# First stage in overlapping rounds, the second stage's weights split at its head, and the last expert's share of the first batch added by products

## The chip, the cores and the metric

The kernel runs on one core of a Trainium2 chip. The metric is the device time of one execution in microseconds, the median of the runs shown; lower is better. TensorE multiplies and transposes into eight PSUM banks, VectorE, ScalarE and GpSimd work element by element (GpSimd works on SBUF alone), and transfers are issued from the queues of SyncE (SP), ScalarE and GpSimd.

## The reference, cut to what matters

Four batches of 512 tokens of 256 numbers pass two decoder layers, six stages in all, each followed by adding the input and a layer norm. The change touches the first four:

```
x = norm(x + spectral(x))       # stage 1: filter from x, bits of a latent, a Golay correction
x = norm(x + gated(x, ctx))     # stage 2: cross attention both ways, weights Wq_c .. Wv_c, Wg
x = norm(x + experts(x))        # stage 3: 8 experts, 512 given tokens each, gelu MLP
x = norm(x + self_attention(x)) # stage 4: rope, 16 heads

# stage 1, per batch, x1 = x @ C, with C a 256x256 matrix from x's extremes and box counts
bits = (x1 @ W_el + b_el > 0); syn = (bits @ H.T > 0.5); w = syn.sum()
bits = where(0 < w <= 3, mod(bits + syn, 2), bits);  y = x1 + bits @ W_le + b_le
# stage 3: out[tok] += weight * (gelu(x[tok] @ W1 + b1) @ W2 + b2), tokens may repeat
```

## The kernel before, in words

Every engine has its own instruction stream, written out in Python, and works through it in order; semaphores (`Signal`, `Bank`) order the engines. X holds all 2,048 tokens in 16 tiles of 128; a batch is 4 tiles (a quarter). Precise products are made from a high and a low part (fp32r pairs), three products for one: ScalarE writes the high part, and VectorE or GpSimd subtracts it for the low part.

**Stage 1** (`spectral`, lines 239 to 528). Small tables and x come in; VectorE finds the extremes (L401, L402) and with a logarithm and sines on ScalarE (L384, L386) the filter, from which TensorE makes C and C W_el (L317, L323). Meanwhile the seven weights of stage 2 pass through two staging buffers (SP, L286, each load behind the subtraction two names earlier), are copied by ScalarE (`take_weights`) and subtracted by GpSimd (L505), three before the rounds and two in each of the next; the context of batch 0 comes last. Then TensorE loops over k = 0 to 4 (L325 on): transposes of batch k+1, latent of batch k (L334), result products of batch k-1 (L344, L345), syndrome (L351) and weight (L354) of batch k. VectorE's loop has bits and flip (L456, L458), threshold (L460), the sums (L466), statistics and aggregates (L472, L476) of batch k-1, three operations of the correction (L480 to L486) and the norm of batch k-1 (L490), for which GpSimd makes the root (L519, L521).

**Stage 2** (`gated`). Before its loop stand the transposes of batch 0 (L596), VectorE's bias scalings, and the split of the source in `take_source(0)` (ScalarE L722, VectorE L814). Then TensorE makes the projections of batch 0 (all L585).

**Stage 3** (`mixture`). Per expert: gather 512 rows, up products with gelu, down products (L1040), weighting (L1200, L1202), a merge product that sums repeated tokens inside a tile of 128 (L1066), its copy (L1172), and a scatter with addition into `acc_scratch` in DRAM (GpSimd, L1231), each scatter behind the one before it. The stage ends with a barrier of all engines but GpSimd.

**Stage 4** (`self_heads`). Wq, Wk, Wv come in through two buffers that rope uses later (SP L1803), ScalarE copies, VectorE subtracts (L1643), then scales bq (L1645) and sets Vone to zero (L1646). The four quarters of the sums are loaded when the last scatter has landed (`norm_loads`, two on each queue), then come statistics, root and norm (`average`, `root`, `norm`) of batch 0, transposes (L1399), copies (L1564), rope (L1664 on VectorE, L1769 on GpSimd), the source's split (L1571, L1672), projections (L1391), and hops over DRAM that bring the heads into rows. GpSimd sets two rows each of rows_q and rows_k (L1772, L1773). Batches 1 to 3 are normed later (`of_next(s, 38)`).

## Time and profile before

| | |
|---|---|
| median of 3 runs | 1976.09 us (1973.51 to 1984.03) |
| the profiled execution's own time | 1980.55 us |
| its span, first to last instruction | 1979.2 us |
| PE, DVE, ACT, POOL busy | 84%, 58%, 51%, 50% of the span |
| mean granted TensorE clock | 0.928 of full speed |

A timeline line gives start, busy time, engine, line, operation, tiles and shapes, and in brackets how long the engine was idle before it and what ended that. Neighbouring instructions of one kind are merged (x4 is four). PE is TensorE's matmul, PEld its weight load, DVE VectorE, ACT ScalarE, POOL GpSimd; ACTq and SPq are the queues that issue transfers. An fp32 product counts as two records. A granted clock of 1.00 is 2.4 GHz and 0.50 is 1.2 GHz.

### The profile page before, as it was taken

The page shows a single profiled execution, that of the slowest core. Times are in us where ns is not written, and L with a number is a line of the kernel's source. Part 1 is how long each engine was busy: PE and PEld are TensorE (multiplying, and loading weights), DVE is VectorE, ACT ScalarE, POOL GpSimd, SP SyncE. Part 2 cuts the span into 40 slices and gives each one's busy share as a digit, 9 for nine tenths or more (in the row PEclk, how much of TensorE's full clock was granted, in tenths as well). Part 3 has the DMA queues.
Part 4 walks back from the last instruction along what each step waited for, and adds up shares of the span by engine and source line. Part 5 has one row for each costly group of instructions (what it writes and reads, how often), then busy time and mean ns, then how long its engine had stood idle before and what let it go on. Part 6 is the DMA issues. An engine that isn't in the chain of part 4 may idle for free. (4 is left out here: it accounts for less than half of the span.)

```text
span 1979.2 us, 23648 instructions
## 1 busy us (share of the span) xinstructions
PE 1667.1 (84%) x7419; PEld 1216.5 (61%) x7419; DVE 1148.9 (58%) x2237; ACT 1012.4 (51%) x1933; POOL 983.2 (50%) x832
## 2 busy tenths in 40 slices
PE   5699994999953897979988999989999997589892
PEld 2387773778842575757655666656666665566661
DVE  4766664666645685858746665655665572542223
ACT  2154442654521485757784776666676673232222
POOL 1200002243324475767873775665675583068885
PEclk9899997999986799999998999999999998579996
DMA  2300103444335222323020111020121120248777
GB/s 83 129 11 1 33 22 101 129 127 133 73 87 137 64 67 64 76 60 81 22 98 15 31 39 31 25 65 23 33 63 26 27 59 19 63 110 192 180 183 173
DMA packets 96785, 146.15 MB, mean 74 GB/s; under 512 B 22711, under 2 KB 61820, under 8 KB 93830
## 3 DMA queue, kind: packets, MB, share of 16 engines
q1 hardware_dynamic: 66448, 104.92, 18.5%
q0 software_dynamic: 18432, 26.36, 7.5%
q10 hardware_dynamic: 11782, 13.37, 2.2%
q8 instruction: 61, 1.00, 0.2%
q14 instruction: 62, 0.51, 0.1%
HBM read 101.83 MB, written 36.41 MB: 70 GB/s over the span
## 5 line engine op out<-in xcount | busy, mean ns | idle before, releaser
L2288 POOL TENSOR_TENSOR STp_lo_use<-ST_use,STp_hi_use 128x512 fp32r<-128x512 f32 x256 | 337.7, 1328 | 201.0 <-ACT ST_use L2118 199.5
L1764 POOL TENSOR_TENSOR STp_lo<-ST,STp_hi 128x512 fp32r<-128x512 f32 x192 | 248.1, 1312 | 104.5 <-ACT ST L1539 103.2
L2183 DVE TENSOR_REDUCE nmax_use<-bank 128x1 f32<-128x512 f32 x256 | 173.6, 680 | 110.0 <-PE bank L2023 105.4
L2114 ACT ACTIVATE STp_hi_use<-bank 128x512 fp32r<-128x512 f32 x256 | 153.1, 598 | 161.0 <-PE bank L2049 157.2
L1657 DVE TENSOR_REDUCE nmax<-bank 128x1 f32<-128x512 f32 x256 | 171.0, 684 | 51.1 <-PE bank L1453 50.2
L1453 PE MATMUL bank<-rows_k,rows_q 65*128 65x512 f32 x256 | 134.8, 535 | 38.8 <-DVE nmax L1657 21.5
L2118 ACT ACTIVATE ST_use<-bank 128x512 f32<-128x512 f32 x256 | 151.7, 593 | 2.0 <-POOL STp_lo_use L2288 2.0
L1536 ACT ACTIVATE STp_hi<-bank 128x512 fp32r<-128x512 f32 x192 | 116.8, 608 | 57.9 <-PE bank L1464 57.4
L2023 PE MATMUL bank<-ks,qs 128*128 128x512 f32 x256 | 110.5, 432 | 10.2 <-DMA ks<-ks 9.6
L1539 ACT ACTIVATE ST<-bank 128x512 f32<-128x512 f32 x192 | 117.8, 613 | 0.0
L951 POOL TENSOR_SCALAR veps<-mv 128x4 f32<-128x4 f32 x4 | 0.9, 228 | 229.2 <-DVE mv L888 229.2
L2730 POOL DMA_INDIRECT acc_scratch<-res,sidx_all x64 | 102.0, 1593 | 24.2 <-issue 17.4
L2033 PE MATMUL bank<-qs,ks 128*128 128x512 f32 x256 | 103.2, 403 | 9.2 <-DMA q<-rowbuf_use 9.0
L1464 PE MATMUL bank<-rows_q,rows_k 66*128 66x512 f32 x256 | 106.3, 415 | 0.9 <-ACT ST L1539 0.8
L2047 PE MATMUL bank<-STp_hi_use,V_hi 128*65 128x512 f32 x256 | 101.5, 397 | 2.2 <-POOL STp_lo_use L2288 2.2
L2712 POOL DMA_INDIRECT rows<-tokens_scratch,gidx_all x64 | 66.4, 1037 | 74.2 <-DVE sidx_all L2604 55.0
L2034 PE MATMUL bank<-q,k 65*128 65x512 f32 x256 | 102.0, 398 | 0.0
L2049 PE MATMUL bank<-STp_lo_use,V_hi 128*65 128x512 f32 x256 | 101.2, 395 | 0.0
L2048 PE MATMUL bank<-STp_hi_use,V_lo 128*64 128x512 f32 x256 | 101.0, 395 | 0.0
L1453 PEld LDWEIGHTS bank<-rows_k,rows_q 65*128 65x128 f32 x256 | 51.6, 203 | 79.5 <-DVE nmax L1657 44.0
L2699 DVE TENSOR_SCALAR res<-bank,rows 128x256 f32<-128x256 f32 x64 | 28.0, 480 | 118.6 <-DMA acc_scratch<-res,sidx_all 110.2
L1121 ACT ACTIVATE hT_hi<-bank,b 128x512 fp32r<-128x512 f32 x64 | 44.1, 689 | 95.1 <-PE bank L1040 91.6
(444 smaller groups left out, 4633.7 us busy)
## 6 DMA issues: line engine op xcount, KB each, us to landing
stage<-in_W SPq DMA_DIRECT2D x16, 1024.0 KB, 4.9
Wgu<-in_Wgu SPq DMA_DIRECT2D x32, 384.0 KB
rows_q<-hop_scratch SPq DMA_DIRECT2D x32, 256.0 KB, 4.4
ks<-ks SPq DMA_DIRECT2D x64, 128.0 KB, 2.3
rinv<-rinv_scratch SPq DMA_DIRECT2D x64, 128.0 KB, 3.0
rows_k<-hop_scratch SPq DMA_DIRECT2D x24, 256.0 KB, 5.4
hop_scratch<-qkp_hi SPq DMA_DIRECT2D x20, 256.0 KB
Wda<-in_Wdn SPq DMA_DIRECT2D x32, 128.0 KB
```

What stands on the lines that cost most here:

```text
L1453: PE.matmul(bk.ap, rows_q[0:MAX_ROW, h, j * P:(j + 1) * P], rows_k[0:MAX_ROW, h, :], start=True, stop=True).then_inc(bk.full, 1)
L1464: PE.matmul(bk.ap, rows_k[:, h, kt * P:(kt + 1) * P], rows_q[:, h, :], start=True, stop=True).then_inc(bk.full, 1)
L1536: A.activation(parts_of(u)[0], bk.ap, ACT.Exp)
L1539: A.activation(ST[u % TB], bk.ap, ACT.Exp).then_inc(bk.free, 1)
L1657: V.tensor_reduce(nmax[:, i % 2, h % HS * TB + j:h % HS * TB + j + 1], bk.ap, AX.X, ALU.max, negate=True).then_inc(bk.free, 1)
L1764: G.tensor_tensor(parts_of(u)[1], ST[u % TB], plain(parts_of(u)[0]), ALU.subtract).then_inc(low.sem, low.inc(u))
L2023: PE.matmul(bk.ap, qs[z][:, j * P:(j + 1) * P], ks[z], start=True, stop=True).then_inc(bk.full, 1)
L2033: PE.matmul(bk.ap, ks[z][:, kt * P:(kt + 1) * P], qs[z], start=True, stop=False)
L2114: A.activation(STp[u % NHI][0], bk.ap, ACT.Exp)
L2118: A.activation(ST[u % NFULL], bk.ap, ACT.Exp).then_inc(bk.free, 1)
L2183: V.tensor_reduce(nmax[:, (h % 2) * TB + j:(h % 2) * TB + j + 1], bk.ap, AX.X, ALU.max, negate=True).then_inc(bk.free, 1)
L2288: G.tensor_tensor(STp[u % NHI][1], ST[u % NFULL], plain(STp[u % NHI][0]), ALU.subtract).then_inc(low["pool"].sem, low["pool"].inc(u))
```

## The change

Stage 1's loop body is cut into functions with the same instructions: `latent`, `syndrome`, `weight` and `result(k, t)` (one tile) on TensorE, `take_bits`, `take_syndrome`, `correct`, `add(k, z)` (two tiles), `average` and `norm` on VectorE. They are put in a new order, in which batch k+1's bits are made between the tiles of batch k. xT has three buffers. Batches 0 and 1 are transposed before the logarithm. The seven weights have a place each, in the staging room of the experts' weights, and all loads are issued at once; GpSimd's subtractions all come behind the filter. Batch 0's transposes and split for stage 2 move into stage 1's rounds 2 and 3, batch 3's statistics and norm into stage 2's first round.

In stage 3, batch 0's sums of experts 0 to 6 are loaded to X while expert 7 runs, and expert 7's share is added by products of a 0/1 matrix `spread` (token of the row against place in the batch) with the weighted rows: three tiles as pairs, the fourth in fp32. The last scatter moves into stage 4. There VectorE does batch 0's statistics and norm between the weights, the memset of Vone is halved, with its second half behind the source's split, and the loads of quarters 1 to 3 are all issued by SP. New tensors: `spread`, `wvp`, `places` (0 to 511).

```diff
@@ -226,17 +226,25 @@
-    kit.names2 = ("Wq_c", "Wk_s", "Wv_s", "Wq_s", "Wk_c", "Wv_c", "Wg")
+    kit.names2 = ("Wk_s", "Wv_s", "Wq_c", "Wq_s", "Wk_c", "Wv_c", "Wg")
-    kit.stage = [sb("stage%d" % z, [P, 2 * DC, D]) for z in range(2)]
+    room = [kit.stage0["W1"].rearrange("p c f -> p (c f)"), kit.stage0["W2"].rearrange("p c d -> p (c d)")]
+    kit.stage2 = {}
+    for n, name in enumerate(kit.names2):
+        size = 2 * DC * D if name == "Wg" else DC * D
+        kit.stage2[name] = room[n // 4][:, n % 4 * DC * D:n % 4 * DC * D + size].rearrange("p (c d) -> p c d", d=D)
-    kit.staged2 = [Signal(kit, "staged%d" % z, range(4), step=16) for z in range(2)]
+    kit.staged2 = [Signal(kit, "staged%d" % z, kit.names2[3 * z:3 + 4 * z], step=16) for z in range(2)]
...
@@ -276,22 +284,25 @@
             for n, name in enumerate(names2):
-                if n > 1:
-                    SP.wait_ge(w_low2.sem, w_low2[names2[n - 2]])
-                SP.dma_start(stage[n % 2][:, 0:2 * DC if name == "Wg" else DC, :], T[name]).then_inc(staged2[n % 2].sem, staged2[n % 2].inc(n // 2))
-            SP.dma_start(kit.ctxT, T["ctxT"][0]).then_inc(kit.ctx_in.sem, kit.ctx_in.inc(0))
+                if n == 3:
+                    SP.dma_start(kit.ctxT, T["ctxT"][0]).then_inc(kit.ctx_in.sem, kit.ctx_in.inc(0))
+                SP.dma_start(stage[name], T[name]).then_inc(staged2[n // 3 > 0].sem, staged2[n // 3 > 0].inc(name))
...
@@ -307,6 +318,7 @@
             turn(0)
+            turn(1)
...
@@ -322,36 +334,57 @@
...
+            latent(0)
+            turn(2)
+            syndrome(0)
+            weight(0)
+            for k in range(B):
                 if k + 1 < B:
+                    latent(k + 1)
+                result(k, 0)
+                result(k, 1)
+                if k + 1 < B:
+                    syndrome(k + 1)
+                if k == 0:
+                    turn(3)
+                if k == B - 2:
+                    turn(0, "next")
+                result(k, 2)
+                if k + 1 < B:
+                    weight(k + 1)
+                result(k, 3)
...
@@ -362,38 +395,37 @@
-                    if b > 1:
-                        A.wait_ge(bank[6].full, bank[6].full_at["y", b - 2])
-                    A.activation(xT[b % 2][:, c, :], bank[c].ap, ACT.Copy).then_inc(bank[c].free, 1)
+                    if b > 2:
+                        A.wait_ge(bank[6].full, bank[6].full_at["y", b - 3])
+                    A.activation(xT[b % 3][:, c, :], bank[c].ap, ACT.Copy).then_inc(bank[c].free, 1)
-                n = names2.index(name)
-                here = stage[n % 2][:, 0:2 * DC if name == "Wg" else DC, :]
-                A.wait_ge(staged2[n % 2].sem, staged2[n % 2][n // 2])
+                here, z = stage[name], names2.index(name) // 3 > 0
+                A.wait_ge(staged2[z].sem, staged2[z][names2[-1 if z else 2]])
...
             a_own = kit.own["act"]
-            take_weights("Wq_c")
-            take_weights("Wk_s")
+            for name in names2[0:3]:
+                take_weights(name)
+            A.wait_ge(kit.ctx_in.sem, kit.ctx_in[0])
+            A.activation(kit.ctxp[0], kit.ctxT, ACT.Copy).then_inc(kit.ctx_high.sem, kit.ctx_high.inc(0))
             take(0)
+            take(1)
...
             A.activation(trig[:, 4:8], trig[:, 0:4], ACT.Sin).then_inc(logged.sem, logged.inc("sines"))
-            take_weights("Wv_s")
-            take(1)
-            take_weights("Wq_s")
-            take_weights("Wk_c")
+            for name in names2[3:]:
+                take_weights(name)
             take(2)
-            take_weights("Wv_c")
-            take_weights("Wg")
-            A.wait_ge(kit.ctx_in.sem, kit.ctx_in[0])
-            A.activation(kit.ctxp[0], kit.ctxT, ACT.Copy).then_inc(kit.ctx_high.sem, kit.ctx_high.inc(0))
...
             take(3)
+            for c in range(DC):
+                A.wait_ge(bank[c].full, bank[c].full_at["next", 0])
+                A.activation(kit.xp[0][:, c, :], bank[c].ap, ACT.Copy).then_inc(kit.src_high2.sem, kit.src_high2.inc((0, "x%d" % c)))
...
@@ -449,47 +481,78 @@
+            V.wait_ge(kit.bias_in.sem, kit.bias_in["bias0"])
+            for d in range(2):
+                V.tensor_scalar(kit.bq[:, d, :], kit.bias0[:, 3 * d, :], D ** -0.5, None, ALU.mult)
+            V.tensor_scalar(kit.bgh, kit.bias0[:, 6, :], 0.5, None, ALU.mult).then_inc(own.sem, own.inc("bias halves"))
...
+            kit.average1, kit.norm1 = average, norm
+            take_bits(0)
+            take_syndrome(0)
+            correct(0)
+            for k in range(B):
+                if k + 1 < B:
+                    take_bits(k + 1)
                 if k:
+                    norm(k - 1)
+                if k == B - 1:
+                    for c in range(DC):
+                        V.wait_ge(kit.src_high2.sem, kit.src_high2[0, "x%d" % c])
+                        V.tensor_tensor(kit.xp[1][:, c, :], bank[c].ap, plain(kit.xp[0][:, c, :]), ALU.subtract).then_inc(bank[c].free, 1)
+                if k + 1 < B:
+                    take_syndrome(k + 1)
+                add(k, 0)
+                if k + 1 < B:
+                    correct(k + 1)
+                add(k, 1)
+                if k + 1 < B:
+                    average(k)
...
@@ -500,21 +563,14 @@
-            for name in names2[0:3]:
+                G.tensor_tensor(W2[name][1], stage[name], plain(W2[name][0]), ALU.subtract).then_inc(w_low2.sem, w_low2.inc(name))
+
+            G.wait_ge(basis_set.sem, basis_set["gbasis"])
+            G.tensor_tensor(kit.ctxp[1], kit.ctxT, plain(kit.ctxp[0]), ALU.subtract).then_inc(kit.ctx_low.sem, kit.ctx_low.inc(0))
+            for name in names2:
                 take_weights(name)
             for b in range(B):
-                if b == 1:
-                    for name in names2[3:5]:
-                        take_weights(name)
-                if b == 2:
-                    for name in names2[5:]:
-                        take_weights(name)
-                    G.wait_ge(kit.ctx_high.sem, kit.ctx_high[0])
-                    G.tensor_tensor(kit.ctxp[1], kit.ctxT, plain(kit.ctxp[0]), ALU.subtract).then_inc(kit.ctx_low.sem, kit.ctx_low.inc(0))
...
@@ -600,6 +658,9 @@
+                    if k == 0:
+                        PE.wait_ge(*kit.source_taken[c])
+                        continue
...
-            turn(0)
...
-            take_source(0)
...
-            take_source(0)
             for k in range(B + 1):
                 if k < B:
                     take_projections(k, 0)
+                if k == 0:
+                    kit.average1(B - 1)
...
                     over_sum(k, 0, TB - 1)
+                if k == 0:
+                    kit.norm1(B - 1)
...
                 if k == 1:
                     SP.dma_start(kit.acc_d[1], bass.AP(T["zeros"].tensor, 0, [[0, (B * S + CAP) * D // 4096], [1, 4096]])).then_inc(kit.zeros_in.sem, kit.zeros_in.inc("zeros"))
+                    SP.wait_ge(w_low.sem, w_low[kit.names2[-1]])
...
             def group(out, pairs):
+                if e == E0 - 1:
+                    spread_out()
                 merge(e, CT0 - 1)
+
+            def spread_out():
+
+                PE.wait_ge(spread_set.sem, spread_set[CT0 - 2])
+                for j in range(TB):
+                    PE.wait_ge(bank[j].free, bank[j].use(("first", j)))
+                    for t in range(CT0 - 1):
+                        for p in range(2):
+                            PE.matmul(bank[j].ap[:, 0:D], spread[:, t, j * P:(j + 1) * P], wvp[p][:, t, :], start=t == 0 and p == 0, stop=False)
+                PE.wait_ge(weighted.sem, weighted[E0 - 1, CT0 - 1])
+                for j in range(TB):
+                    PE.matmul(bank[j].ap[:, 0:D], plain(spread[:, CT0 - 1, j * P:(j + 1) * P]), wv[(CT0 - 1) % 2], start=False, stop=True).then_inc(bank[j].full, 1)
...
+            for t in range(CT0 - 1):
+                A.wait_ge(weighted.sem, weighted[E0 - 1, t])
+                A.activation(wvp[0][:, t, :], wv[t % 2], ACT.Copy).then_inc(wv_high.sem, wv_high.inc(t))
...
+            def find_places(t):
+
+                if t == 0:
+                    V.wait_ge(tok_in[0].sem, tok_in[0]["places"])
+                m = V.tensor_scalar(spread[:, t, :], tok_row[0], tok_col[:, (E0 - 1) * CT0 + t:(E0 - 1) * CT0 + t + 1], None, ALU.is_equal)
+                if t == CT0 - 1:
+                    m.then_inc(spread_set.sem, spread_set.inc("places"))
+
+            def take_low(t):
+                V.wait_ge(wv_high.sem, wv_high[t])
+                V.tensor_tensor(wvp[1][:, t, :], wv[t % 2], plain(wvp[0][:, t, :]), ALU.subtract).then_inc(spread_set.sem, spread_set.inc(t))
...
+                else:
+                    for t in range(CT0):
+                        find_places(t)
...
                     if t > 1:
                         V.wait_ge(bank[6 + t % 2].full, bank[6 + t % 2].full_at["merge", e, t - 2])
+                        if e == E0 - 1:
+                            V.wait_ge(spread_set.sem, spread_set[t - 2])
...
                     if t:
                         take_merged(e, t - 1)
+                        if e + 1 == E0:
+                            take_low(t - 1)
+                if e + 1 == E0:
+                    V.wait_ge(first_in.sem, first_in["s3"])
+                    for j in range(TB):
+                        V.wait_ge(bank[j].full, bank[j].full_at["first", j])
+                        V.tensor_tensor(X[:, j, :], bank[j].ap[:, 0:D], X[:, j, :], ALU.add).then_inc(bank[j].free, 1)
                 take_merged(e, CT0 - 1)
...
-                for t in range(CT0):
+                for t in range(CT0 - (e == E0 - 1)):
                     bk = bank[6 + t % 2]
                     G.wait_ge(bk.free, bk.free_at["merge", e, t])
+                    if e == E0 - 1 and t == 0:
+                        G.wait_ge(first_in.sem, first_in["s3"])
...
+            SP.wait_ge(own.sem, own["again", E0 - 2])
+            SP.dma_start(tok_row[0], bass.AP(T["places"].tensor, 0, [[0, P], [1, S]])).then_inc(tok_in[0].sem, tok_in[0].inc("places"))
+            SP.wait_ge(stored.sem, stored[E0 - 2, CT0 - 1])
+            SP.dma_start(X[:, 0:TB, :], acc_d[0:S].rearrange("(t p) d -> p t d", p=P)).then_inc(first_in.sem, first_in.inc("s3"))
...
+        last = bank[6 + (CT0 - 1) % 2]
+        kit.last_merged = last.free, last.free_at["merge", E0 - 1, CT0 - 1]
+        kit.first_added = [(bank[j].free, bank[j].free_at["first", j]) for j in range(TB)]
...
-            norm_loads(A, (1, 3))
...
         def average(k):
-            V.wait_ge(kit.quarter_in[k].sem, kit.quarter_in[k]["s3"])
+            if k:
+                V.wait_ge(kit.quarter_in[k].sem, kit.quarter_in[k]["s3"])
             for t in range(NT)[quarter[k]]:
+                if k == 0:
+                    V.wait_ge(*kit.first_added[t])
...
@@ -1638,14 +1753,19 @@
-            for n, name in enumerate(names):
...
+            average(0)
+            take_weights(0)
+            norm(0)
+            take_weights(1)
+            take_weights(2)
             V.wait_ge(kit.tables_in.sem, table)
             V.tensor_scalar(bq, bqkv[:, 0, :], HD ** -0.5, None, ALU.mult).then_inc(own.sem, own.inc("s4 bias"))
-            V.memset(plain(Vone), 0.0).then_inc(own.sem, own.inc("s4 V"))
-            average(0)
-            norm(0)
+            V.memset(plain(Vone[:, 0:TB // 2]), 0.0)
...
+                if of_next(s, 26) == 0:
+                    V.memset(plain(Vone[:, TB // 2:TB]), 0.0).then_inc(own.sem, own.inc("s4 V"))
...
@@ -1751,8 +1873,12 @@
         def pool():
+            root(0)
+            G.wait_ge(*kit.last_merged)
+            G.wait_ge(kit.stored0.sem, kit.stored0[E0 - 1, CT0 - 2])
+            G.indirect_dma_start(kit.acc_d[0], bass.IndirectOffsetOnAxis(ap=kit.last_sidx[:, CT0 - 1:CT0], axis=0), summed[:, CT0 - 1, :], None,
+                                 compute_op=ALU.add).then_inc(kit.stored0.sem, kit.stored0.inc((E0 - 1, CT0 - 1)))
             G.wait_ge(kit.tables_in.sem, table)
-            root(0)
...
-            norm_loads(SP, (0, 2))
+            norm_loads(SP, (1, 2, 3))
```

## Rows read from the trace of the kernel before

**Rows 1.** Busy time by stretch: length, PE, PEld, DVE, ACT, POOL, granted clock, DMA share, GB/s.

```profile
98.00:108.00 10.00, 10.00 (x48) 8.38 (x48) 3.59 (x5) 3.36 (x5) 0.00 (x0) 0.84 0.01 2
...
637.00:690.00 53.00, 45.14 (x121) 26.82 (x122) 36.75 (x62) 22.02 (x41) 18.42 (x14) 0.68 0.31 74
```

**Rows 2.** Timeline of the first stage: start, length, engine, operation, idle before.

```profile
21.01 0.20 ACT L384 ACTIVATE mm<-mm 5x1 f32<-5x1 f32 x1 [1.28 <-DVE mm L425]
...
43.06 1.13 PE L344 MATMUL bank<-Cmat,xT 128*128 128x256 f32 x4
...
50.34 1.02 PE L354 MATMUL bank<-syn,golay 128*24 128x512 f32 x2 [0.86 <-DVE syn L460]
...
51.29 1.09 PE L298 MATMUL bank<-ident,X 128*128 128x128 f32 x8
...
52.31 1.90 PE L334 MATMUL bank<-xT,CW 128*24 128x512 f32 x4
...
55.28 1.13 PE L344 MATMUL bank<-Cmat,xT 128*128 128x256 f32 x4 [1.07 <-DVE corr L486]
...
67.38 6.38 DVE L490 TENSOR_SCALAR X<-summed,mv,rstd 128x256 f32<-128x256 f32 x4
...
68.55 2.39 POOL L505 TENSOR_TENSOR w_Wg_lo<-stage,w_Wg_hi 128x1024 fp32r<-128x1024 f32 x1
...
73.80 0.74 DVE L456 TENSOR_SCALAR bits<-bank,b_el 24x512 f32<-24x512 f32 x1
...
93.93 1.38 DVE L490 TENSOR_SCALAR X<-summed,mv,rstd 128x256 f32<-128x256 f32 x4 [1.47 <-POOL rstd L521]
...
97.78 0.76 PE L585 MATMUL bank<-xp_hi,w_Wq_c_hi 128*128 128x512 f32 x1 [6.97 <-DVE xp_lo L814]
```

**Rows 3.** Groups of instructions from 31 to 97.7 us; mean ns of one after the comma.

```profile
L466 DVE TENSOR_TENSOR summed<-bank,X 128x256 f32<-128x256 f32 x16 | 5.7, 405 | 6.5 <-PE bank L345 6.5
...
L472 DVE BATCH_NORM_STATS2 stats<-summed 128x6 f32<-128x256 f32 x16 | 5.5, 402 | 0.0
...
L482 DVE TENSOR_TENSOR fix<-fix,flip 24x512 f32<-24x512 f32 x4 | 2.7, 678 | 0.1
...
L458 DVE TENSOR_SCALAR flip<-bits 24x512 f32<-24x512 f32 x4 | 1.7, 414 | 0.1
...
L476 DVE BATCH_NORM_AGGREGATE mv<-stats 128x2 f32<-128x6 f32 x16 | 1.5, 157 | 0.1
...
L814 DVE TENSOR_TENSOR xp_lo<-bank,xp_hi 128x512 fp32r<-128x512 f32 x2 | 1.3, 686 | 0.7 <-ACT xp_hi L722 0.7
```

**Rows 4.** Timeline in the second stage, first batch.

```profile
116.15 0.74 DVE L830 SCALAR_TENSOR_TENSOR Q_lo<-bank,bq,Q_hi 128x512 fp32r<-128x512 f32 x1
...
118.00 0.39 PE L585 MATMUL bank<-ctxp_hi,w_Wq_s_hi 128*128 128x512 f32 x1
```

**Rows 5.** The last expert's last 24 products alone, from the windows.

```profile
568.20:571.30 3.10, 3.03 (x24) 3.00 (x24) 1.00 0.39 42
```

**Rows 6.** Timeline from the last expert into the self-attention stage.

```profile
562.05 0.42 DVE L1200 TENSOR_TENSOR wv<-bank,b 128x256 f32<-128x256 f32 x1 [3.25 <-PE bank L1040]
...
572.58 0.67 PE L1066 MATMUL bank<-wv,same 128*128 128x256 f32 x2 [0.65 <-DVE wv L1202]
...
573.97 0.64 SPq L1803 DMA_DIRECT2D turned<-in_Wq  x1
...
584.99 0.16 DVE L1645 TENSOR_SCALAR bq_use<-bqkv 128x2 f32<-128x2 f32 x1
...
586.80 6.88 DVE L1646 MEMSET Vone<- 128x8192 f32 x1 [1.65 <-issue]
...
599.59 0.60 ACT L1564 ACTIVATE xT<-bank 128x512 f32<-128x512 f32 x1 [15.24 <-PE bank L1399]
...
602.02 2.36 DVE L1664 TENSOR_TENSOR turned<-xT,cs 128x512 f32<-128x512 f32 x2 [3.70 <-ACT xT L1564]
...
605.56 6.92 POOL L1772 MEMSET rows_q<- 2x8192 f32 x1
```

182 lines of the change are left out of this document (94 added, 88 removed).

## The prediction

> **What bounds the kernel now.** The busy shares of the whole span say little here, because the change touches two short stretches, so I read the stretches in order of time. The timeline of the first stage shows four rounds, one per batch, each a ladder between TensorE and VectorE: TensorE makes the latents, VectorE turns them into bits, TensorE the syndrome, VectorE a threshold, TensorE the weight, VectorE three operations of 0.68 us [rows 3], and only then come TensorE's result products. Those start at 43.06 for batch 0 and at 55.28 for batch 1 [rows 2], so a round takes 12.2 us, and neither engine is full in it. The third round is worse: VectorE's norm of batch 1, 1.38 us when nothing disturbs it, takes 6.38 us at 67.38, beside GpSimd's subtraction of Wg at 68.55, and the bits of batch 3 wait until 73.80 [rows 2]. After the last result products come, one after another, the sums, the statistics, a 1.47 us detour over GpSimd, the norm, the transposes of batch 0 and their split. The second stage's first product starts at 97.78, after 6.97 us of idle TensorE [rows 2]. From there TensorE is busy without a gap, at a granted clock of 0.84 [rows 1].
>
> The second stretch runs from the last expert to the first rope operation of self-attention. After the last expert's products nothing runs but a chain of transfers: four scatters one after the other, then the loads of the sums, then statistics, norm and transposes of batch 0. Wq's load is issued at 573.97, VectorE's memset of Vone takes 6.88 us from 586.80, batch 0's first turned half is copied at 599.59, and rope starts at 602.02 [rows 6].
>
> **First stage.** Terms from one profiled execution (1980.55 us by its own time, 1979.2 us of span; 4.5 us above the median of 1976.09).
> - *Head.* ScalarE now does four weight activations, the context's split and batches 0 and 1 before the logarithm, where two weights and one batch stood. The logarithm ran at 21.01 and waited 1.28 us for VectorE [rows 2], so that much of the addition is free; I put the rest at 1.2 us. It is bounded by 0 and by 4 us (seven operations of 0.6 us, as the copy in rows 6). In return, latent(0) doesn't stand behind turn(1) any more (1.09 us at the full clock), but turn(2) now stands before syndrome(0). I take batch 0's result products at 43.5, for 43.06 [rows 2]; between 42.5 and 47.
> - *Rounds.* TensorE has per round latents 1.90, syndrome and weight 1.02 each, and twelve 256-column result products; two of them are 1.13 us and overlap the next, so twelve are about 5.3 [rows 2]. That is 9.2, and 1.1 more in rounds 0 and 2 for eight transposes. VectorE has bits 0.74, flip 0.41, norm 1.38, threshold 0.68, four sums of 0.405, three corrections of 0.68, four statistics of 0.40 and four aggregates of 0.16 [rows 2, 3]: 9.1 by the records, about 8.7 as these overlap, and waits of 0.3 (the 1.47 us detour less bits and flip) and 0.5 (the weight product less two sums), so 9.5. Hence result starts of 43.5, 53.8 and 63.3.
> - *End.* In round 2 the weight of batch 3 is done 7.1 us after that start (two tiles 2.65, syndrome, transposes, one tile 1.3, weight), at 70.4; corrections to 72.5. Then VectorE is what ends last: sums 0.8, statistics and aggregates 2.0, detour 1.5, norm 1.4, and the split of the source, two of 0.686 [rows 3], give 79.6. TensorE's last products end at 77.8, before that. The first product of the second stage moves from 97.78 to 79.6: **18.2 us** less. The transposes of batch 0 and ScalarE's half of the split are in round 2, the bias scalings beside latent(0), the last batch's statistics and norm in the second stage.
> - *Clock.* A granted 0.84 over 10 us [rows 1] is 3.2 us at 1.2 GHz, after 6.97 us of idling; at 2.4 GHz it would be 1.6 less. With 1.8 us of idling in place of 7 and full rounds before it, I take **1.6** (0 to 1.6).
> - *Second stage.* VectorE gets batch 3's statistics and aggregates (about 1.8) before its first peak and the norm (1.4) before the second direction's projections. The first shifts a chain that waits on the scores by 1.3, the second adds to it: 2.7 us. Q_lo ends at 116.89 and TensorE needs its bank at 118.00 [rows 4], so 1.1 us of it is hidden, and TensorE stands **1.6 us** (0.6 to 3.2). Behind that wait stand the second half of the projections, and the peaks behind those.
> - *Transfers and GpSimd.* SP issues all weights and the context at once and waits for nothing, so 4.5 MB are under way at the head; the input is first in that queue, and only the ScalarE term above depends on what is behind it. The first expert's weights now wait for the last subtraction, which by these sums is over at about 38 us, long before the third stage. All of GpSimd's subtractions lie behind the filter's basis and beside TensorE's filter and latent products: cost nil, and the 5 us that two norms lost at 67.38 go away (they are in the 18.2).
>
> On that last point the row shows that a VectorE operation with SBUF operands alone, beside a GpSimd subtraction, took five times its length [rows 2]. The Trainium skill (SBUF — State Buffer, section on the two separate sides) says why: VectorE and GpSimd share one port pair under an exclusive lock, and who starts first keeps it for the whole instruction. By that rule the three bias scalings and the flip of batch 0, which the change puts beside the subtractions, would each wait for one; I took nothing for them. The same rule bears on the new memset, below.
>
> **Last expert.** The load of batch 0's sums leaves after expert 6's last scatter, while expert 7's up products run; GpSimd's first scatter of expert 7, which now waits for it, is only ready behind the first down product (562.05 [rows 6]) and its merge. The four comparisons, if as long as another 128x512 operation (0.69 [rows 3]), are 2.7 us and fit the 3.25 us in which VectorE idles before 562.05 [rows 6]. ScalarE's copies and VectorE's splits of the first two tiles fit the 3 us between tiles. On the path stand: VectorE's third split (done at 573.2), 24 products, which take 3.03 us at the full clock [rows 5], four fp32 products of 256 columns (0.67 one by one [rows 6], half of the 1.02 of a 512-column product back to back [rows 2]; I take 0.5, so 2.0), the last merge 0.67 and its copy with the hand-over 0.5. The stage's end, and with it Wq's load, moves from 573.97 to 579.5, by **5.5 us** (4.5 to 7). From there the old chain "Wq, Wk, Wv split, then bq" holds with its 11.0 us, so bq stands at 590.5 (before 584.99) [rows 6]. Batch 0's statistics, root and norm fit between its links, and its transposes are done by then; the last scatter and the loads of batches 1 to 3 are no longer ahead of anything before the averages, 20 us on. After bq ScalarE copies the turned halves: from 599.59 to 602.02 it was 2.43 us, so 593.1. VectorE's memset, now half (3.44 from the 6.88 in rows 6), ends at 594.1 and is later than that. Rope moves from 602.02 to 594.1: **7.9 us** less. The second half of the memset stands behind the source's split, beside the first projection, and costs nothing if it runs at once. Lower bound 5, upper 9.
>
> **Sum.** 18.2 + 1.6 - 1.6 + 7.9 = 26.1 us less. All stages follow one another, so it reaches the end: 1980.55 - 26.1 = 1954.5 for the profiled execution, and by the median 1976.09 - 26.1 = **1950.0**. A measurement here can tell about 0.5% (10 us) from no change; the gain is 1.3%.
>
> **Rivals.**
> 1. *The rounds stay a ladder.* The head's copies come late (the weights' share of a semaphore covers three transfers), or VectorE's order makes TensorE wait for threshold and correction in each round, 11.5 us per round in place of 9.5 to 10.3. For: VectorE is at 9.5 of 9.6 us, with no slack. Against: bits and norms are taken one round apart. Then some 7 us are lost: 1957. Chance 0.15.
> 2. *The last expert's part gives nothing.* The barrier's 5.5 us delay is certain, the gain isn't: if Wv's load is slowed by the scatter and the 1.5 MB of sums, now beside it, bq is later by as much. Then 18.2 + 1 remain: 1957. Chance 0.09.
> 3. *The port.* GpSimd's memset of rows_q takes 6.92 us from 605.56 [rows 6], from about 597 in the changed kernel; if VectorE's second memset has to wait for its end at 604, it ends at 607.5, and the first hop is 2.3 us later; the bias scalings and the flip cost up to 1.3. That gives 1953.6. The exclusive lock of the page named above is the rule for it, if a memset takes the pair; no row shows two memsets together. Chance 0.10.
> 4. *Slower.* The self-attention loop starts at a low clock: 0.68 over 53 us from 637 [rows 1], which is 34 us at 1.2 GHz, with TensorE busy for 45 of them. What starts a stretch earlier also moves where TensorE idles between batches. Each further stretch of that sort costs 17 us, so two give back more than the gain (about +8) and three end at 2001. It decides from 36 us more of lost clock on. Against: nothing in that loop is changed. Chance 0.02.
>
> That the change doesn't do what it says (stage by stage later by the moved work) is held in 1 and 2. The rest, 0.64, is the forecast. The range takes in 1 to 3, the bounds of the head (3.5 late), the second stage and the end, and a spread like that of the runs before (1973.51 to 1984.03): 1944 to 1963. Faster by over 0.5% needs 1966 or less: 0.92; within 0.5%: 0.05; slower: 0.03.
>
> **What would show it.** In the changed kernel's timeline: result products about 9.5 to 10.3 us apart, no norm over 1.5 us, the second stage's first product at 79.6 (78 to 84) with under 2.5 us of idling before it, and a granted clock of 1.00 behind it; TensorE waiting for Q_lo about 1.6 us; Wq's load 5.5 us after the last expert's old end; rope about 26 us earlier than 602.02. Wrong would be the rounds' step if they were still 11 us or more apart, and the last one if rope gained no more there than the first stage did.

## The result, and the profile after

The changed kernel takes 1948.95 us (median of 4 runs, 1945.63 to 1955.06) beside 1976.05 (1973.51 to 1984.03) before: ratio 0.9859, 95% interval 0.9833 to 0.9884. It is 27 us faster, forecast were 26. The profiled execution took 1955.06 us (span 1953.7), 25.5 us less than that of before. Of the executions below, two (2043.63 us of the kernel with the old order, 2544.32 us of the changed kernel) ran slow as a whole, at a mean granted clock of 0.81 and 0.62, and no ratio counts them.

The first stage in the timeline of the changed kernel (start and duration in us; in brackets the idle time before it and what ended it): the logarithm, the first result product of each batch, VectorE's norms, the second stage's first products.

```profile
22.43 0.20 ACT L419 ACTIVATE mm<-mm 5x1 f32<-5x1 f32 x1
32.83 3.58 PE L343 MATMUL bank<-xT,CW 128*24 128x512 f32 x4 [0.35 <-issue]
36.52 0.74 DVE L492 TENSOR_SCALAR bits<-bank,b_el 24x512 f32<-24x512 f32 x1 [1.92 <-PE bank L343]
43.32 1.13 PE L364 MATMUL bank<-Cmat,xT 128*128 128x256 f32 x4 [0.48 <-DVE corr L508]
53.69 1.13 PE L364 MATMUL bank<-Cmat,xT 128*128 128x256 f32 x4
56.45 1.38 DVE L531 TENSOR_SCALAR X<-summed,mv,rstd 128x256 f32<-128x256 f32 x4 [0.41 <-POOL rstd L577]
60.01 0.68 DVE L502 SCALAR_TENSOR_TENSOR fix<-bank,syn 24x512 f32<-24x512 f32 x1 [0.81 <-PE bank L354]
63.23 1.13 PE L364 MATMUL bank<-Cmat,xT 128*128 128x256 f32 x4
70.38 0.68 DVE L502 SCALAR_TENSOR_TENSOR fix<-bank,syn 24x512 f32<-24x512 f32 x1 [1.63 <-PE bank L354]
72.54 1.13 PE L364 MATMUL bank<-Cmat,xT 128*128 128x256 f32 x4 [0.70 <-DVE corr L508]
77.76 1.29 DVE L547 TENSOR_TENSOR xp_lo<-bank,xp_hi 128x512 fp32r<-128x512 f32 x2
79.15 0.47 PE L643 MATMUL bank<-xp_hi,w_Wq_c_hi 128*128 128x512 f32 x1 [1.17 <-DVE xp_lo L547]
```

Rounds of 10.37, 9.54 and 9.31 us stand where [rows 2] had 12.2 and more, the norm of 6.38 us is gone, and the second stage starts at 79.15 for 97.78: 18.6 us. Its first product takes 0.47 us for the 0.76 of a half clock, and from there to the first scores it is 8.84 us (79.15 to 87.99) where it was 10.47 (97.78 to 108.25): 1.6 more. Two rows of the windows view, of the changed kernel (columns as in [rows 1]), show the full clock behind that first product and, at the end of the second stage, a stretch at a mean of 0.88 in which 1.5 us went again. The timeline has the first products of that stretch:

```profile
79.15:82.00 2.85, 2.85 (x12) 2.33 (x13) 1.63 (x5) 0.69 (x1) 0.00 (x0) 1.00 0.03 6
274.00:302.00 28.00, 21.19 (x85) 15.98 (x83) 12.28 (x26) 9.85 (x18) 1.27 (x2) 0.88 0.11 38
```

```profile
294.36 0.79 PE L643 MATMUL bank<-cTp_hi,w_Wg_hi 128*128 128x512 f32 x1 [3.07 <-DVE cTp_lo L905]
294.95 0.63 PE L643 MATMUL bank<-cTp_lo,w_Wg_hi 128*128 128x512 f32 x1
```

At 288 us the changed kernel is 19.9 us ahead (its last weights are turned at 287.6, before at 307.5); then, behind 3.07 us of idle TensorE, the first seven of the last 24 gate products run at the half clock (0.63 us each), where the kernel before, behind the same 3.07 us, had them at 0.39, and at the last gate activation (301.67 for 320.09) it is 18.4 ahead.

The last expert and the head of self-attention, changed kernel:

```profile
540.34 1.67 DVE L1258 TENSOR_SCALAR spread<-tok_row,tok_col 128x512 fp32r<-128x512 int32 x4
554.68 0.38 PE L1152 MATMUL bank<-wvp_hi,spread 128*128 128x256 f32 x1 [1.14 <-DVE wvp_lo L1264]
557.65 1.89 PE L1155 MATMUL bank<-wv,spread 128*128 128x256 f32 x8
560.69 0.64 SPq L1929 DMA_DIRECT2D turned<-in_Wq  x1
569.68 0.63 ACT L1633 ACTIVATE Wk_hi<-part 128x512 fp32r<-128x512 f32 x1 [4.96 <-DMA part<-in_Wk]
572.86 0.16 DVE L1767 TENSOR_SCALAR bq_use<-bqkv 128x2 f32<-128x2 f32 x1
573.81 3.47 DVE L1768 MEMSET Vone<- 128x4096 f32 x1 [0.79 <-issue]
577.20 2.29 DVE L1784 TENSOR_TENSOR turned<-xT,cs 128x512 f32<-128x512 f32 x2
580.67 6.92 POOL L1898 MEMSET rows_q<- 2x8192 f32 x1
585.34 3.47 DVE L1794 MEMSET Vone<- 128x4096 f32 x1 [0.80 <-issue]
```

Rope stands at 577.20 for 602.02, 24.8 us ahead, so this part gave 6.7 us. Counted from the third stage's start, taken as the first ScalarE rounding of its hidden tiles (330.46; before 348.59), Wq's load leaves 230.2 us behind it (before 225.4) and rope starts 246.7 us behind it (253.4). From there to the end only 0.7 us is added.

### The profile page after: what moved, and what is told of

The parts are those of the page before. It is cut to its first block and busy times, and to the rows that moved or that the text cites. A ratio compares the mean times of both kernels' runs of the same rounds, so it can differ in the third digit from the quotient of the medians.

```text
span 1953.7 us, 23728 instructions
## 1 busy us (share of the span) xinstructions
PE 1667.5 (85%) x7451; PEld 1216.7 (62%) x7451; DVE 1146.5 (59%) x2249; ACT 1012.8 (52%) x1936; POOL 985.7 (50%) x832
## 3 DMA queue, kind: packets, MB, share of 16 engines
q1 hardware_dynamic: 67648, 106.23, 18.8%
```

## The experiments

There were twelve runs of nine kernels, each beside the kernel before. A program's runs scatter by some 10 us, so what the edits do is mostly read from the traces, between two instructions of one execution.

### The halves alone

The change's diff was cut at the mixture: the first stage and the second as changed with the rest as before, the mixture and the head of self-attention as changed with the rest as before, and the changed kernel itself. All three were measured twice, each time beside the kernel before. What the first half leaves out, in its core:

```diff
-                if e == E0 - 1:
-                    spread_out()
                 merge(e, CT0 - 1)
...
-                for t in range(CT0 - (e == E0 - 1)):
+                for t in range(CT0):
```

> The changed first and second stages with the last expert and the head of self-attention as before. My theory: all of the first stage's gain is its own. First product of the second stage at 79 (before 97.8) after about 1.2 us of idle TensorE, at the full clock; first scores another 1.6 earlier against it than before (clock); then 0.3 lost in the heads. So 19.9 us less by the last turned weights of the second stage; the rest of the kernel as before: 1956 us, ratio 0.990. The changed kernel also showed a low-clock stretch on the last gate products, which took 1.6 back. Theory A: that was where the throttle happened to fall, so this kernel may or may not show it and the sum of the two halves' gains is that of the whole. Rival B: the change moves TensorE's pauses so that it always falls there: then 18.3 less, 1957.7, with products of 0.63 us at the gate again. Rival C: the two halves lean on each other (a gain of the first stage is partly waited off at the last expert): then under 17 less.

> The first and second stages of before, with batch 0's share of the last expert added by products, the load of its sums before the last scatters, and the memset in halves. My theory: 6.4 us less, as in the changed kernel: Wq's load 5.1 later against the last expert than before (near 579.1), the first rope operation near 595.6 (before 602.0), 1969.7 us, ratio 0.9968. The first product of the second stage stands at 97.8 and runs at half the full clock after 7 us of idle TensorE. In the changed kernel Wk and Wv took 8.3 and 6.1 us to land where 7.0 and 4.9 stood. Theory A: the last scatter, which now leaves 3.5 us after Wq's load in place of 1.4, is beside them: they land as late here. Rival B: it was chance of that execution: they land in 7.0 and 4.9 here, and rope is near 594.5. Rival C: nothing is gained (the barrier comes as much later as the tail is shorter): 1976.

> The changed kernel itself, so that the others of this call have it on the same chip: ratio 0.984 to 0.988. What its second trace tells: whether the low-clock stretch on the last gate products (product 0.63 us, 1.6 us lost against the kernel before) and the loads of Wk and Wv (8.3 and 6.1 us to land, before 7.0 and 4.9) come again. If they are of the change, both do; if chance, they differ.

> First and second stages changed, the rest as before, once more beside the whole change and the other half, since the first measurement left open whether the halves add up: 0.9917 and 0.9988 for the halves, a sum of 18.8 us, against 0.9864, 26.8 us. The traces say 19 to 20 us for this half. If they add up, this gives 0.990 and the two halves together come within 3 us of the whole. Rival: the whole gives more than its parts (a stretch at a low clock that only the whole avoids): again under 20 in sum.

> The last expert's part alone, once more. The traces put rope 7.3 us earlier against the third stage's start (246.2 us behind the mixture's first hidden tile, 253.4 in the kernel before) and the forecast said 7.9: ratio 0.9963. The first measurement gave 0.9988 with an interval up to 1.0008. Theory A: that was the scatter of the runs, and this gives 0.995 to 0.998. Rival: the self-attention loop, which starts earlier and with less idling behind it, gives 4 us back in low-clock stretches in every execution: 0.998 to 1.000 again, and in its trace the loop from the first maximum to the end is 3 us or more longer than 1341.3.

> The whole change, once more in the same call as its halves: 0.985 to 0.988, 24 to 29 us less.

| series | first stage alone | last expert alone | whole change |
|---|---|---|---|
| first | 0.9917 (0.9886 to 0.9947) | 0.9988 (0.9968 to 1.0008) | 0.9864 (0.9832 to 0.9896) |
| second | 0.9927 (0.9902 to 0.9952) | 0.9976 (0.9953 to 0.9999) | 0.9886 (0.9849 to 0.9923) |

Of about 1975 us the halves give 18.8 us in sum in the first series (whole 26.8) and 19.2 in the second (whole 22.5). The second pair agrees within its intervals, the first only at their edge; whether the whole gives a few us more than its parts stays open.

In the traces nothing of the kind is seen: the first half alone has its second stage's first product 42.6 us behind batch 0's bits, as the whole, in both executions, and in the last expert's part alone rope stands 246.2 and 245.7 us behind the first hidden tile. It is rather the halves of which the runs give less than the traces: 16.4 and 14.4 us for the first, which by the traces is worth 18 to 20, and 2.4 and 4.7 us for the last expert, which by them is worth 7.3 and 7.7. In three of the four the interval holds the traces' value; what the fourth lacks (at most 6.3 us for 7.3) is not shown. It is not the self-attention loop in every execution: from its first maximum to the end it took 1343.7 and then 1340.2 us with the last expert's part (before 1341.3), so it does not give back 3 us every time, and that rival falls.

Two questions of the first trace remain. The last gate activation comes 158.1, 159.5 and 156.5 us behind the first one in three executions of the changed kernel (before 156.8): the low stretch there comes and goes with one and the same program. The traces of all kernels leave open whether the change makes it more frequent: with the new first stage, edited or not, it is 158.1 us or more in seven of eleven executions, with that of before in one of three (156.8, 156.6, 158.4). The other is chance: from Wq's load to bq it is 12.2, 11.0 and 11.1 us in them (before 11.0), so Wk's late landing in the first was not the last scatter's doing.

### GpSimd's subtractions back beside the norms

```diff
-            for name in names2:
+            for name in names2[0:3]:
                 take_weights(name)
             for b in range(B):
+                if b == 1:
+                    for name in names2[3:5]:
+                        take_weights(name)
+                if b == 2:
+                    for name in names2[5:]:
+                        take_weights(name)
```

> The changed kernel with one edit: GpSimd subtracts the 4th and 5th weights of the second stage before batch 1's root and the last two before batch 2's, as before the change, and not all seven ahead of batch 0's. My theory: VectorE sets the rounds and has no slack, and a norm beside a GpSimd subtraction waits for it: norms of 4 to 6.5 us in place of 1.38 in two rounds, and the first product of the second stage at 84 to 89 in place of 79.2, the whole 5 to 10 us above the changed kernel (1954 to 1959). Rival A: rounds are set by TensorE, VectorE's longer norms are hidden: first product at 79 to 81, time within 2 us of the changed kernel. Rival B: the roots of batches 1 and 2 wait behind the subtractions on GpSimd, which costs more than the port: idle before the norms over 2 us while the norms themselves stay at 1.4.

Ratio 0.9915 (0.9880 to 0.9949). That is 11 us above the changed kernel of the same series (0.9864). Its timeline:

```profile
52.62 1.26 POOL L567 TENSOR_TENSOR w_Wq_s_lo<-stage,w_Wq_s_hi 128x512 fp32r<-128x512 f32 x1
52.68 3.27 DVE L531 TENSOR_SCALAR X<-summed,mv,rstd 128x256 f32<-128x256 f32 x4 [0.41 <-POOL rstd L583]
53.84 1.32 POOL L567 TENSOR_TENSOR w_Wk_c_lo<-stage,w_Wk_c_hi 128x512 fp32r<-128x512 f32 x1
57.87 0.68 DVE L502 SCALAR_TENSOR_TENSOR fix<-bank,syn 24x512 f32<-24x512 f32 x1 [0.54 <-PE bank L354]
63.85 4.36 DVE L531 TENSOR_SCALAR X<-summed,mv,rstd 128x256 f32<-128x256 f32 x4 [0.41 <-POOL rstd L583]
70.13 0.68 DVE L502 SCALAR_TENSOR_TENSOR fix<-bank,syn 24x512 f32<-24x512 f32 x1 [0.54 <-PE bank L354]
```

The norms take 3.27 and 4.36 us for 1.38, 4.9 us more, and each ends 0.8 us behind GpSimd's pair of subtractions, as it would if the norm waited for both. From the first result product (39.55) to the last batch's (72.29) it is 32.7 us, for 29.2 in the changed kernel: 3.5 us arrive. The other 1.4 had cover: in the changed kernel VectorE idles 0.81 and 1.63 us for TensorE's weight product, here 0.54 and 0.54. So VectorE did have slack, though only 1.4 us of it. Counted from batch 0's bits (33.57) to the second stage's first product (78.90) the loss seems smaller, 45.3 us for 42.6, but the 0.8 us between are the head's clock: this execution has its transposes there at the full clock (1.09 us for eight), the changed kernel's at half of it (1.93). The 3.5 us by the trace are less than my theory's 5 to 10, and than the 11 by the runs, whose intervals hold both.

### The order inside the rounds back

```diff
-                result(k, 0)
-                result(k, 1)
+                for t in range(TB):
+                    result(k, t)
                 if k + 1 < B:
                     syndrome(k + 1)
+                    weight(k + 1)
...
-                result(k, 2)
-                if k + 1 < B:
-                    weight(k + 1)
-                result(k, 3)
...
-                if k:
-                    norm(k - 1)
...
                 add(k, 0)
-                if k + 1 < B:
-                    correct(k + 1)
                 add(k, 1)
                 if k + 1 < B:
                     average(k)
+                    correct(k + 1)
+                    norm(k)
```

> The changed kernel with the order inside its rounds put back: TensorE makes all four tiles of result products and then syndrome and weight, VectorE takes the sums and statistics ahead of the corrections and norms the batch in its own round. GpSimd's subtractions stay early, the last batch's statistics stay in the second stage, and the transposes and split of the second stage's source stay beside the last round. It splits the 18.7 us by which the first stage is shorter. My theory: rounds of 11.3 to 12.2 us in place of 10.4, 9.5 and 9.3, so the last result products start 4 to 6 us later against the first (29.2 us there), and the first product of the second stage 4 to 5 us later against batch 0's bits (42.6 us there: 46.5 to 48). Then of the 18.7, some 4 to 5 are the order inside the rounds, 2.7 the subtractions (as their own run showed), and 11 what left the end of the stage. Rival A: the order inside the rounds is most of it: 52 or more. Rival B: it is worth nothing without the subtractions beside: 43 to 44.

Ratio 0.9906 (0.9870 to 0.9943). Its timeline:

```profile
36.39 0.74 DVE L489 TENSOR_SCALAR bits<-bank,b_el 24x512 f32<-24x512 f32 x1 [0.69 <-PE bank L343]
43.23 1.13 PE L364 MATMUL bank<-Cmat,xT 128*128 128x256 f32 x4 [0.48 <-DVE corr L505]
55.46 1.13 PE L364 MATMUL bank<-Cmat,xT 128*128 128x256 f32 x4 [1.07 <-DVE corr L505]
67.68 1.13 PE L364 MATMUL bank<-Cmat,xT 128*128 128x256 f32 x4 [2.21 <-DVE corr L505]
69.28 1.91 PE L364 MATMUL bank<-Cmat,xT 128*128 128x256 f32 x4
81.60 1.21 PE L364 MATMUL bank<-Cmat,xT 128*128 128x256 f32 x4 [2.91 <-DVE corr L505]
83.45 1.91 PE L364 MATMUL bank<-Cmat,xT 128*128 128x256 f32 x4
88.38 0.58 PE L638 MATMUL bank<-xp_hi,w_Wq_c_hi 128*128 128x512 f32 x1
```

Bits to first product: 52.0 us for 42.6, rival A almost to the decimal. The order alone is worth 9.4 us, and about 3.4 of that is clock: TensorE now idles 2.21 and 2.91 us for the corrections, and behind each pause four products take 1.91 us for 1.03. The third round is 13.92 us for 12.22, and the last four tiles take 7.1 for 5.4. By the runs it is 0.9906 beside 0.9886 for the changed kernel of the same series, about 4 us, with intervals that hold 9.4.

The other half of the 18.7 us between [rows 2] (61.3 from bits to first product) and the changed kernel stands at the stage's end. Two more lines of the kernel before:

```profile
67.51 1.13 PE L344 MATMUL bank<-Cmat,xT 128*128 128x256 f32 x4 [0.65 <-DVE corr L486]
81.51 2.07 PE L344 MATMUL bank<-Cmat,xT 128*128 128x256 f32 x4 [3.92 <-DVE corr L486]
```

From the last batch's first result product to the second stage's first product it was 16.3 us there, and is 6.8 with the old order and 6.6 in the changed kernel: 9.5 us left with the last batch's statistics and norm and the transposes and split of the source, 1.3 of them because its last four tiles, behind 3.92 us of idling, lost still more to the half clock (8.4 us for 7.1). The three rounds ahead of that took 38.5 us before, 38.4 with the old order and 29.2 in the changed kernel. So in the old order the early subtractions gained nothing in these rounds: the third, 14.00 us behind a norm of 6.38, is 13.92 with a norm of 1.36, because the half clock took what the norm gave back. The 3.5 us of the subtractions hold for the new order and are not a third part of the 18.7. The moves at the stage's end were not run by themselves.

### The last batch's norm back in the first stage

```diff
-                if k + 1 < B:
-                    average(k)
+                average(k)
+                if k == B - 1:
+                    norm(k)
```

and the two calls in the second stage taken out.

> The changed kernel with the last batch's statistics, aggregates and norm put back behind its sums at the end of the first stage's program, in place of before the second stage's first peak and projections. In the changed kernel TensorE waited 0.27 us for Q_lo where I had forecast 1.6. My theory: VectorE then stands until about 85 us (statistics 1.8, root 1.5, norm 1.4 after its sums end at 80.4), the splits of the first Q and K wait, and the first scores (88.0 in the changed kernel, 8.84 us after the first product) come 1.5 to 3.5 us later against the first product; 1.3 of it comes back because the peaks and projections behind them have no foreign work. The gate's first activation, 64.4 us behind the first product in both executions of the changed kernel, is at 65 to 67. Rival (the forecast's term): placed in the second stage the work costs 1.6 us of TensorE, placed here it is free: the gate at 62.8.

Ratio 0.9886 (0.9841 to 0.9931). Its timeline:

```profile
84.98 0.75 DVE L884 SCALAR_TENSOR_TENSOR Q_lo<-bank,bq,Q_hi 128x512 fp32r<-128x512 f32 x1
85.78 0.79 PE L644 MATMUL bank<-xp_hi,w_Wq_c_hi 128*128 128x512 f32 x1 [2.25 <-DVE Q_lo L884]
86.38 0.63 PE L644 MATMUL bank<-xp_lo,w_Wq_c_hi 128*128 128x512 f32 x1
```

TensorE waits 2.25 us for the split of the first Q, and behind the wait products take 0.63 us for 0.39. The gate's first activation is 67.8 us behind the first product, for 64.4, above my theory's 65 to 67: against this place the move into the second stage gains 3.4 us.

### Ahead of rope

The memset between the norm and Wk's split; three of the five tables (Wo, bo, bv) issued behind the last weight's rounding; and both together, with the context's and Wq_c's rounding in the first stage put behind the sines.

```diff
             norm(0)
+            V.memset(plain(Vone[:, 0:TB // 2]), 0.0)
             take_weights(1)
...
-            V.memset(plain(Vone[:, 0:TB // 2]), 0.0)
```

> The changed kernel with one edit: VectorE's first memset of Vone stands between the norm of batch 0 and the split of Wk, where VectorE idled 3.6 us, and not behind bq. My theory: that memset is what ends last ahead of rope, and ScalarE's second copy of the turned halves is next, 1.7 us before it. So the rope operation starts 2.6 us after bq (4.34 in the changed kernel, in two executions), and all behind it is 1.7 us earlier; Wk's split is not delayed by more than 0.2. Rival A: the copies end last: 4.3 us as before, nothing gained. Rival B: the memset, 3.47 us long, meets a Wk that lands in 6.7 us and not in 8.3, so the split of Wk waits up to 1.5 us and bq with it: the gain is 0.2 to 1. Over the whole run 1.7 us is below what the rounds can tell; the trace decides.

```diff
-            for n, (dst, src) in enumerate(tables):
+            for n in range(2):
...
                 A.activation(W[name][0], stage[n % 2], ACT.Copy, scale=scale.get(name, 1.0)).then_inc(w_high.sem, w_high.inc(name))
+            A.wait_ge(kit.tables_in.sem, first_tables)
+            for n in range(2, len(tables)):
+                A.dma_start(*tables[n]).then_inc(kit.tables_in.sem, kit.tables_in.inc(("s4", n)))
```

> The changed kernel with one edit: of the five tables that ScalarE's queue loads at the head of self-attention (1.02 MB) only bqkv and cs (0.5 MB) are issued beside Wq; Wo, bo and bv follow behind the last weight's rounding. My theory: Wk and Wv land late because 1.5 MB are under way together; in the changed kernel's two executions Wk took 8.3 and 6.7 us to land and Wv 6.1 and 5.0. Here Wk takes 4 to 5.5 and Wv about 4, bq stands 9 to 10 us behind Wq's issue (12.2 and 11.0 there), and rope is 1 to 3 us earlier. Rival: the delay is that of a load itself on this queue: Wk and Wv land as before and nothing moves.

```diff
-            for name in names2[0:3]:
+            for name in names2[0:2]:
                 take_weights(name)
-            A.wait_ge(kit.ctx_in.sem, kit.ctx_in[0])
-            A.activation(kit.ctxp[0], kit.ctxT, ACT.Copy).then_inc(kit.ctx_high.sem, kit.ctx_high.inc(0))
...
             A.activation(trig[:, 4:8], trig[:, 0:4], ACT.Sin).then_inc(logged.sem, logged.inc("sines"))
+            A.wait_ge(kit.ctx_in.sem, kit.ctx_in[0])
+            A.activation(kit.ctxp[0], kit.ctxT, ACT.Copy).then_inc(kit.ctx_high.sem, kit.ctx_high.inc(0))
-            for name in names2[3:]:
+            for name in names2[2:]:
```

> Meant to beat both. The changed kernel with three edits: the memset between norm and Wk's split, the three large tables behind the last weight's rounding, and in the first stage the context's rounding and that of Wq_c behind the logarithm and the sines. My theory: the logarithm is at 21.0 to 21.3 us (22.4 in the changed kernel), result products 1.2 us earlier against the input's arrival; bq 9.5 to 11 us behind Wq's issue and rope 2.6 behind bq, so rope 12 to 13.5 us after Wq's issue in place of 15.3 to 16.5. Together 3.5 to 5 us less than the changed kernel: about 1944 beside its 1949. Rival A: the memset now delays the split of the earlier Wk, and of the second pair of gains at most 1 us is left: 1947. Rival B: GpSimd's subtractions start later by the two roundings and reach into the norms: rounds over 10.5 us and nothing gained in the first stage.

| | ratio (interval) | Wq's load to bq | bq to rope | load to rope |
|---|---|---|---|---|
| changed, three executions | | 12.2, 11.0, 11.1 | 4.3 | 16.5, 15.3, 15.4 |
| memset between | 0.9875 (0.9831 to 0.9918) | 11.4 | 2.6 | 14.0 |
| tables later | 0.9867 (0.9823 to 0.9910) | 10.0 | 4.3 | 14.4 |
| both, and the head | 0.9843 (0.9804 to 0.9882) | 12.2 | 2.6 | 14.9 |

The memset did end last: moved, it gives 1.7 us, of which Wk's split takes some back. The tables did hold up the weights: without three of them Wk is rounded 5.6 us behind Wq's load, for 9.0 in the changed kernel's first execution and 7.4 in its second. Together they gain least, as rival A said, by a row of the combined kernel:

```profile
568.29 0.63 ACT L1634 ACTIVATE Wk_hi<-part 128x512 fp32r<-128x512 f32 x1 [0.72 <-DMA part<-in_Wk]
570.38 3.47 DVE L1768 MEMSET Vone<- 128x4096 f32 x1 [0.80 <-issue]
573.77 0.63 DVE L1763 SCALAR_TENSOR_TENSOR Wk_lo<-part,Wk_hi 128x512 fp32r<-128x512 f32 x1
```

Wk is rounded by 568.9, and its split waits for the memset until 573.8. The logarithm stands at 21.85, 0.6 us earlier, not 1.2, and the kernel with the tables later, whose first stage is unchanged, has it at 21.83: the head's part shows nothing. The median of this kernel, 1949.74 us, is no better than the changed kernel's, so none is shown to beat it.

## Why the prediction was right or wrong

**First stage, 18.2 forecast, 18.6 measured.** Result starts came at 43.3, 53.7, 63.2 and 72.5 for 43.5, 53.8, 63.3 and 72.5, the first product at 79.15 for 79.6. One reason in the working was wrong: that VectorE "is at 9.5 of 9.6 us, with no slack". It waits for TensorE's weight product 0.81 and 1.63 us in two of the rounds, and 4.9 us of longer norms cost 3.5. Nor do "the 5 us that two norms lost at 67.38" explain much of the gain: beside that norm stood three subtractions, not Wg's alone, and the old order without them had a third round as long (13.92 us for 14.00). The start of 43.5 was right for a pair of profiles with the same slow head (below); the sizes of the order and of the stage's end are from the runs.

**Clock, 1.6.** Measured 1.63 up to the first scores. Not in the sum: the low stretch at the gate, 1.5 lost in the profiled execution and in others not.

**Second stage, 1.6 forecast, about 0.6 measured** (first scores to the gate's first activation: 55.6 us for 55.0). Here a step failed: "The first shifts a chain that waits on the scores by 1.3, the second adds to it." Rows of the changed kernel:

```profile
88.99 1.40 DVE L521 BATCH_NORM_STATS2 stats<-summed 128x6 f32<-128x256 f32 x4
91.41 0.69 ACT L806 ACTIVATE prob<-bank,nmax 128x512 f32<-128x512 f32 x1 [1.76 <-DVE nmax L889]
95.74 0.49 DVE L896 TENSOR_SCALAR prob<-prob,rinv 128x512 f32<-128x512 f32 x1
96.14 1.38 DVE L531 TENSOR_SCALAR X<-summed,mv,rstd 128x256 f32<-128x256 f32 x4
98.36 0.50 PE L643 MATMUL bank<-ctxp_hi,w_Wq_s_hi 128*128 128x512 f32 x1 [0.27 <-DVE Q_lo L883]
```

The first exponential is 1.0 us later against the first scores (3.42 us for 2.39), but at the fourth row block's scaling only 0.25 of it is left (7.75 for 7.50): the chain had pauses that the delay used up. Only the norm's 1.4 stands before Q_lo, 1.1 of it is hidden as forecast, and TensorE waits 0.27 us.

**Last expert, 7.9 forecast; 6.7 in the profiled execution, 7.7 and 7.9 in the two others.** Spreading products took 2.97 us for 3.0, the fp32 ones 1.89 for 2.0, the comparisons 1.67 for 2.7. The stage's end moved by 4.9 for 5.5. Against that, bq to the end of the memset was put at 3.6 us and is 4.3: the 0.8 us ahead of a memset that follows bq, which [rows 6] show as 1.65, was left out. In the profiled execution 1.2 us more are Wk's landing.

**Rivals.** The rounds did not stay a ladder (1), and the last part gave its gain (2). Of the port (3) both halves can be read. Three small operations did wait beside GpSimd's subtractions, in the changed kernel:

```profile
32.64 0.81 DVE L486 TENSOR_SCALAR bq<-bias 128x2 f32<-128x2 f32 x2
33.37 1.23 DVE L487 TENSOR_SCALAR bgh<-bias 128x2 f32<-128x2 f32 x1
37.29 1.09 DVE L494 TENSOR_SCALAR flip<-bits 24x512 f32<-24x512 f32 x1
```

Undisturbed they take 0.24, 0.16 and 0.41. All of it lies beside the latents and the transposes of batch 2, so it cost nothing, as taken. The memset's half of the rival did not occur: the second half of Vone ran its 3.47 us from 585.34, beside GpSimd's memset of rows_q, behind 0.8 us. The Trainium skill (SBUF — State Buffer, section "Who interferes with whom") says that a VectorE instruction with at most one SBUF input, outside the two-port modes, does not contend with GpSimd; the memset agrees with that, and I had overlooked it when I gave this rival its 0.10. The self-attention loop (4) took 1340.1 us from its first maximum to the end for 1341.3, and gave nothing back.

**The sum.** In the profiled pair: 18.6 + 1.6 - 0.6 up to the first gate (19.7 by the rows), 1.3 lost to the gate's clock, 0.3 to the routing, 6.7 gained, 0.7 behind: 25.5 for the forecast 26.1. The mechanisms of the three large terms held, but that the total came within 1 us is partly luck: of the errors of about 1 us each the second stage and the stretch behind rope helped, the last expert and the gate's clock (which no term had) hurt, and runs of one kernel differ by 10 us.

## What to carry to other kernels

Where two engines hand one batch back and forth, interleaving the next batch's short chain with this one's long products paid twice here: the waits went, and with them the pauses behind which TensorE ran at half its clock (3.4 of the 9.4 us). Work of the last batch that nothing needs at once belongs in the next stage's first pause, if VectorE has one there; in front of that stage's first split it cost 3.4 us. Put a movable VectorE operation only into a gap whose length the loads do not set: the memset fitted the gap before Wk's split until Wk came early.

## What the runs showed of the hardware

The head, the same instructions in each program, differs by 3 us and more from execution to execution. From the logarithm to batch 0's bits the kernel before took 15.5 us, and the kernel with the last expert's part alone, the same program there, 12.1 and 14.2. The rows of the latents, of the kernel before and of that one, show half of it (the products and transposes ahead of them the other):

```profile
32.77 3.61 PE L334 MATMUL bank<-xT,CW 128*24 128x512 f32 x4
```

```profile
31.04 1.90 PE L334 MATMUL bank<-xT,CW 128*24 128x512 f32 x4
```

A factor of two is what the half clock would give, yet the windows view has the granted clock at 1.00 for both, first the kernel before and then the other:

```profile
32.00:34.00 2.00, 2.00 (x6) 0.76 (x6) 0.00 (x0) 1.71 (x3) 0.00 (x0) 1.00 0.00 0
31.00:33.00 2.00, 1.94 (x6) 0.33 (x4) 0.00 (x0) 1.97 (x5) 0.00 (x0) 1.00 0.00 0
```

That it is the clock is inferred: the eight transposes ahead are longer in proportion (1.95 us for 1.07), and so are the eight small products that make C W_el (1.90 for 1.07), and no other cause is seen. So in this stretch the duration of a known product is the safer reading, and the recorded clock doesn't tell the two apart. Among eleven executions of the changed head the latents took 1.9 us in two, 2.7 to 2.8 in three and 3.2 to 3.6 in six. Both profiles of the first comparison happened to have the slow form, which is why their first stages could be set against each other; a pair of unlike ones would have been off by 3 us, a sixth of what was to be explained.
